# A graph kernel in two layers: window 0 weighed ahead of the weights, and another order for the last two windows of layer 1

## The reference

```python
# layer 0: attention over the edges, 4 heads of 16, with h = relu(layernorm(x))
ZU = einsum('nd,kdr->knr', Z, U)
logits = (ZU[:, src] * ZU[:, dst]).sum(-1) / sqrt(R)
alpha = softmax of logits over the edges of one target
agg = segment_sum(alpha * ZU[:, src], dst)
ssa = einsum('k,knr,kdr->nd', softmax(head_w), agg, U)
...                         # two products with Dmat, relu
x = x + that
# layer 1: h = relu(layernorm(x))
msg = h[src] + relvectors[kind]
red = segment_sum(msg, dst)
x = x + gru_cell(red, h, w_ih, w_hh, b_ih, b_hh)
```

## Time and profile before

| | us |
|---|---|
| median of three runs | 1041.13 |
| the three runs | 1041.29, 1037.07, 1041.13 |
| the profiled execution, its own time | 1040.8 |
| its span | 1038.9 |

### The profile page before, as it was taken

How to read it: one execution, slowest core, us unless ns; L and a number is a source line. 1 busy time by engine, 2 the same in 40 slices (tenths; PEclk the granted TensorE clock), 3 DMA queues, 4 the chain that set the end, 5 groups by cost and what they waited for, 6 DMA issues and landing times.

```text
span 1038.9 us, 14242 instructions
## 1 busy us (share of the span) xinstructions
PE 875.4 (84%) x4828; PEld 686.0 (66%) x4828; DVE 633.3 (61%) x1285; ACT 416.4 (40%) x804; POOL 626.1 (60%) x969
## 2 busy tenths in 40 slices
PE   6833688897888977888888966689999999999996
PEld 5732676776777755777777754466666776777774
DVE  5341577799977777877777744443233433388853
ACT  5423216565655545555565543322211111124441
POOL 4698888888888888888888888881010010000000
PEclk9956557689886777866786887856999999999999
DMA  9361335545655544544454443313344344421111
GB/s 200 70 166 37 77 70 132 130 118 143 158 150 123 118 119 116 139 118 118 120 137 121 118 101 90 92 43 83 105 137 127 122 120 136 125 84 50 51 51 37
DMA packets 54646, 112.99 MB, mean 109 GB/s; under 512 B 15435, under 2 KB 32968, under 8 KB 51443
## 3 DMA queue, kind: packets, MB, share of 16 engines
q1 hardware_dynamic: 34632, 81.38, 24.2%
q0 software_dynamic: 18880, 30.57, 17.8%
q10 hardware_dynamic: 1056, 0.07, 0.1%
HBM read 80.99 MB, written 30.86 MB: 108 GB/s over the span
## 4 chain that ended last, share of the span: by engine, by line
POOL 54%; PE 34%; issue 7%; DVE 1%; SPq 1%; DMA 1%; ACT 1%; ACTq 0%; POOLq 0%; DVEq 0%
POOL shared L725 27%; POOL zs_third L725 13%; POOL cnt_rows L730 13%; PE bank L1957 13%; PE bank L1956 6%; PE bank L1983 5%; PE bank L1984 2%; PE bank L1833 1%; PE bank L1883 1%; PE bank L1934 1%; PE bank L1808 1%; PE bank L1711 1%; PE bank L1980 1%; PE bank L1975 1%; DMA xs<-in_x 1%
## 5 line engine op out<-in xcount | busy, mean ns | idle before, releaser
L725 POOL DMA_INDIRECT shared<-zu_table,src_col x306 | 301.2, 984 | 52.0 <-issue 48.8
L1808 PEld LDWEIGHTS bank<-zus,shared 125*128 125x128 f32 x900 | 148.1, 260 | 15.9 <-issue 14.4
L1808 PE MATMUL bank<-zus,shared 125*128 125x64 f32 x900 | 148.8, 345 | 8.8 <-ACT shared L1519 5.9
L725 POOL DMA_INDIRECT zs_third<-zu_table,src_col x144 | 141.0, 979 | 23.0 <-issue 23.0
L1000 DVE TENSOR_TENSOR setup<-iota_b,bank 128x500 bf16<-128x500 bf16 (+1 forms) x252 | 139.9, 607 | 8.1 <-PE bank L1920 7.9
L1833 PE MATMUL bank<-layer,oh 128*125 128x84 f32 x900 | 144.2, 338 | 0.0
L730 POOL MEMSET cnt_rows<- 54x240 f32 x450 | 142.6, 317 | 0.3
L1833 PEld LDWEIGHTS bank<-layer,oh 128*125 128x125 f32 x900 | 141.6, 254 | 0.3 <-issue 0.3
L1920 PE MATMUL bank<-setup 128*125 128x125 bf16 x450 | 52.2, 253 | 39.7 <-DVE setup L1000 38.8
L1574 ACT ACTIVATE setup<-bank 125x500 bf16<-125x500 f32 (+1 forms) x126 | 77.5, 678 | 12.2 <-PE bank L1920 11.5
L1920 PEld LDWEIGHTS bank<-setup 128*125 128x125 bf16 x450 | 45.9, 164 | 53.4 <-DVE setup L1000 47.0
(11 more groups left out here) (235 smaller groups left out, 1692.2 us busy)
## 6 DMA issues: line engine op xcount, KB each, us to landing
shared<-in_edges SPq DMA_DIRECT2D x25, 1125.0 KB
counts_table<-setup SPq DMA_DIRECT2D x18, 683.6 KB
own_table<-own_out SPq DMA_DIRECT2D x25, 375.0 KB
shared<-own_table SPq DMA_DIRECT2D x25, 375.0 KB
zus<-counts_table POOLq DMA_DIRECT2D x9, 683.6 KB, 5.3
shared<-counts_table POOLq DMA_DIRECT2D x9, 683.6 KB, 5.0
shared<-zu_table,src_col POOLq DMA_INDIRECT x306, 3.9
h_table<-h2s SPq DMA_DIRECT2D x25, 125.0 KB
```

The source lines that it names most:

```text
L725: nc.gpsimd.indirect_dma_start(out=zs[t % 3][:, j * KR:(j + 1) * KR], out_offset=None, in_=zu_table, in_offset=bass.IndirectOffsetOnAxis(a ...
L1808: last = mm(ps(c, 128, (j - a) * KR, (j - a + 1) * KR), ohT[:, j * 128:(j + 1) * 128], zus[:, t, :], start=True, stop=True)
```

## The change

- **The start.** `attend_first` takes the place of `attend(0)`. It weighs window 0 and adds its means before the GRU weights are turned; weights, relation products and biases stand behind. SyncE loads the rows of group 1 (windows 5 to 11) right behind window 0, then windows 1 and 2, then the weights. The edge rows of groups 2 and 3 are loaded in halves in windows 2 to 5 and turned behind `attend(4)` and `attend(6)`. The keys are turned in banks 5, 6 and 7, where they were turned in 0, 1 and 2.
- **The end.** `attend_next_to_last(23)` and `attend_last(24)` have orders of their own on PE, DVE and ACT. VectorE finishes window 23 (its sums divided, its means, the new x, the shift) ahead of chunks 1 and 2 of the logits of window 24. TensorE puts blocks 0 to 17 of the sums of window 0 of layer 2 into window 23, and the others into window 24.
- **For that,** the counts of window 0 have a buffer of their own, `first_many`, loaded by SyncE behind the prefetch for window 24. The sums of windows 0 and 1 go to banks 0 and 1, and the third gate of window 22 goes to the half of bank 6 that is free. GpSimd waits for the last gathers of window 24 before it loads the counts of window 1.

```diff
+        first_many = narrow(part(W, SPAN, SPAN))
...
+            def load_first_counts():
+                sp.wait_ge(oht_made, NW - 1)
+                sp.wait_ge(st_counts, 32 * AHEAD)
+                for lo, hi in SIXTEENTHS:
+                    sp.dma_start(first_many[lo:hi, :], counts_table[lo:hi, :]).then_inc(l_first, 16)
...
                 load_window(0, 0)
+                load_rows(sp, 1, early_rows, GROUPS[1][1])
                 load_window(1, 1)
+                load_window_behind(0, 0)
                 load_gru()
-                load_rows(sp, 1, early_rows, GROUPS[1][1])
-                load_rows(sp, 2, *GROUPS[2])
-                load_rows(sp, 3, *GROUPS[3])
...
-                load_counts(0)
+                pool.wait_ge(g_zs[(NW - 1) % 3][2], 16 * (CHUNKS[2][1] - CHUNKS[2][0]) * ((NW - 1) // 3 + 1))
                 load_counts(1)
...
+            def attend_next_to_last(t, h):          # VectorE
+                differ(t)
+                weigh_rows(t, h)
+                find_cuts(t // 2 + h, 1 - h)
+                one_hots(t + 1, 1 - h)
+                logits(t + 1, t // 2 + h, 1 - h, 0)
+                shift(t - 1)
+                dve.wait_ge(agg_made, t + 1)
+                weigh(t, ps(5, W, 0, SUMS))
+                remainder(t - 1, 1 - h)
+                keep_means(t)
+                relation_one_hots(t + 1)
+                rest_of_rows(t - 1)
+                renew(t)
+                shift(t)
+                logits(t + 1, t // 2 + h, 1 - h, 1)
+                remainder(t, h)
+                logits(t + 1, t // 2 + h, 1 - h, 2)
+                scan(t + 1, 1 - h)
+                find_most(t + 1)
+                rest_of_rows(t)
...
+            def attend_next_to_last(t):             # TensorE
+                pe.wait_ge(x1_made, 2 * t - 1)
+                dense_part(t)
+                target_rows(t + 1)
+                sum_rows(t, t % 2)
+                turn_own(t - 1)
+                sum_blocks(0, 0, 2)
+                turn_means(t)
+                sum_blocks(0, 2, 3)
+                add_means(t)
+                turn_row(t + 1)
+                sum_blocks(0, 3, 4)
+                pe.wait_ge(x1_made, 2 * t + 1)
+                all_own_products(t - 1)
+                sum_blocks(0, 4, 9)
+                turn_logits(t + 1)
+                sum_blocks(0, 9, 13)
+                turn_most(t + 1)
+                sum_blocks(0, 13, 18)
+
+            def attend_last(t):
+                pe.wait_ge(hTw_kept, t + 1)
+                sum_rows(t, t % 2)
+                pe.wait_ge(own_kept, 2 * t - 2)
+                dense_part(t)
+                turn_own(t - 1)
+                turn_means(t)
+                sum_blocks(0, 18, 19)
+                add_means(t)
+                all_own_products(t - 1)
+                sum_blocks(0, 19, NW)
+                pe.wait_ge(own_kept, 2 * t)
+                turn_own(t)
+                sum_blocks(1, 0, 5)
+                all_own_products(t)
```

More of the change, by code:

```diff
@@ L485, in fives_of, with sum_bank, own_third @@
             return i * NW // 5, (i + 1) * NW // 5
-        def overlapped(step):
-            for t in range(NW):
-                step(t, t // 2, t % 2, t == 0, t == NW - 1)
+        def sum_bank(t):
+            return (5, 7)[t % 2] if t >= 2 else t
+        def own_third(t):
+            return ps(6, W, D, 2 * D) if t == NW - 3 else ps(2, W, 0, D)
         def way(eng, windowed, by_blocks):
@@ L1090, in first_logits, with columns_as_numbers @@
             def first_logits():
-                for c in range(3):
-                    logits(0, 0, 0, c)
+                logits(0, 0, 0, 0)
+                columns_as_numbers(1)
+                logits(0, 0, 0, 1)
+                logits(0, 0, 0, 2)
                 scan(0, 0)
                 find_most(0)
-            def attend(t, i, h, first, last):
+            def columns_as_numbers(g):
+                a, b = GROUPS[g]
+                dve.wait_ge(l_rows[g], 16 * (b - a))
+                block = late_rows[:, (a - FIRST) * 128:(b - FIRST) * 128]
+                nc.vector.tensor_copy(block, block.bitcast(int32)).then_inc(v_rowf, 1)
@@ new lines, in attend_first @@
+            def attend_first():
+                differ(0)
+                weigh_rows(0, 0)
+                find_cuts(0, 1)
+                one_hots(1, 1)
+                logits(1, 0, 1, 0)
+                dve.wait_ge(agg_made, 1)
+                weigh(0, ps(5, W, 0, SUMS))
+                keep_means(0)
+                relation_one_hots(1)
+                renew(0)
+                biases()
+                dve.wait_ge(v_bias, 3)
+                three_parts(bfull[:, :], bias3, 0)
+                logits(1, 0, 1, 1)
+                logits(1, 0, 1, 2)
+                scan(1, 1)
+                find_most(1)
+                dve.wait_ge(a_relw, 3)
+                three_parts(relw_low[:, :], low3, 5)
@@ L1111, in attend @@
                     pairs_of(t - 1, 1)
-                if not last:
-                    logits(t + 1, i + h, 1 - h, 2)
+                logits(t + 1, i + h, 1 - h, 2)
                 dve.wait_ge(agg_made, t + 1)
                 weigh(t, ps(5, W, 0, SUMS))
-                if not first:
-                    remainder(t - 1, 1 - h)
-                if not last:
-                    scan(t + 1, 1 - h)
+                remainder(t - 1, 1 - h)
+                scan(t + 1, 1 - h)
                 if pairs:
@@ L1462, in cuts, with exponentials @@
                 nc.scalar.activation(cutf[:, h, 1:HALO], cut[:, h, 1:HALO], ACT.Copy, scale=-BIG).then_inc(cut_made, 1)
-            def attend(t, i, h, first, last):
+            def exponentials(t):
                 act.wait_ge(dif_made, t + 1)
@@ L1493, in attend @@
                     keep_staged(t - 1, 2)
-                if not last:
-                    keep_turned(t + 1)
+                keep_turned(t + 1)
                 if counts:
@@ L1828, in attend, with all_own_products, sum_rows @@
+            def all_own_products(t):
+                relation_products_of_own(t)
+                for c in range(CH):
+                    own_products(t, c)
+            def sum_rows(t, h):
                 pe.wait_ge(oh_made, t + 1)
@@ L1967, in gru @@
                 more = t + 1 < NW
-                sum_blocks(t, LEAD if t else NW - 1, NW)
-                if more:
+                if t:
+                    sum_blocks(t, LEAD, NW)
+                if t and more:
                     sum_blocks(t + 1, 0, 5)
```

311 lines of the change are left out of this document (181 added, 130 removed).

## The result

The changed kernel takes 1030.29 us, median of seven runs (1027.24 to 1050.65); the kernel before took 1041.01, median of seven in the same comparison (1037.07 to 1041.29). The ratio is 0.9898, with a 95% interval of 0.986 to 0.9936: 1.0% faster, where I had forecast 0.25% and put 1038.5 us. The range, 1026.5 to 1043, holds the time, but only by the part of it that rival A had been given: the forecast's own range, 1036.5 to 1042, does not.

What follows compares the result with a forecast made beforehand. GpSimd's gathers bound layer 1, TensorE layer 2. Start 0; end steps -1.1 us (741.4 against 742.53), a load +0.5, an earlier clock -1.5: -2.1 from 1040.8, about 1038.5 us, range 1026.5 to 1043.

Steps and rivals of the forecast that it cites:

- rival A: End of layer 1: clock full from about 690, first GRU begins at 729.3, 13.2 us sooner, 1027.6 us; chance 0.22.
- What bounds the kernel: Layer 1 runs as long as GpSimd needs for 450 gathers; TensorE bounds layer 2, going block to block without a gap.
- the start: Window 0 brought forward, weights, biases and edge rows behind it: gains nothing while GpSimd sets the pace, 0 us (-1 to +1).
- within 1 us of 703: Sign for the start: GpSimd's last gather still ends there; if sooner, the reading of the start is wrong.
- The steps at half clock up to the first turning: Steps 1 to 6 at the end of layer 1: first GRU begins at 741.4 against 742.53, -1.1 us.
- The two transfers: Count loads near the last gathers: GpSimd's moved away, 1.4 us sooner but worth nothing at half clock; SyncE's added, +0.5 us.
- a clock that rises sooner: End of layer 1: full clock 3 us before the guess in the logits' turning is worth -3 us; taken as -1.5.
- the end of the account: The comparison stopped at the first GRU, begun at 742.53 before; work behind it was taken as the same in both kernels.
- if layer 2 loses its dense row of blocks to late loads: Sign that the forecast is wrong, at the start of layer 2; no size given.
- the likeliest case: The forecast itself, with half clock at the end of layer 1: 1037 to 1041.5 us, chance 0.5.
- B: Clock comes back at about 709, amid the logits' turning; GRU begins at 737.9, -4.6 us, 1036 us; chance 0.15.
- C: VectorE's order is the bound, clock half until about 728; GRU begins at 746 to 747, +4, 1045 us; chance 0.1.

Runs made afterwards that it cites:

- paced pair: Kernel before and changed kernel, each with a second clearing of the idle rows behind each of 450 gathers: 1196.14 us and 1186.49 us.
- paced_start: The changed start with the order of before at the end, plus a second clearing of idle rows behind each gather: 1195.57 us, six runs.
- paced_after: The whole changed kernel plus a second clearing of idle rows behind each gather: 1186.49 us, six runs.
- paced_before: The kernel before plus a second clearing of idle rows behind each gather: 1196.14 us, six runs.
- again: The changed kernel rerun with no edit, for another profile: 1205.3 us against 1199.17 of the kernel before on chip 2, ratio 1.0196.

## Why the prediction came out as it did

**What bounds the kernel, and the start: right.** GpSimd waited for no window, and the start is worth 0.6 us in the paced pair, within the scatter. The last gather ended 1.1 us sooner (1.4 in paced_start), which by my own sign ("within 1 us of 703") would speak against this reading. It doesn't: the gathers were shorter one by one (439.8 us in sum for 442.2), and GpSimd had no wait before that could have gone away.

**The steps at half clock up to the first turning: right to about 1 us each.** The profile after is such a run. Counted from the division of window 23: last logits after 8.3 us (720.41; forecast 9.4), their turning after 12.3 (12.7), from there to the division of window 24 8.7 (8.8), to the first turning 12.8 (13.6). Together -2.4 us against before; the forecast had -1.1.

**The two transfers: wrong sign or nothing.** Counts loaded beside the last gathers cost nothing: in the paced pair the last chunk is taken 2.54 us after the last gather with them (859.06 to 861.60) and 2.53 without (857.59 to 860.12). SyncE's load of the first counts did not delay window 23 either: in the profile after it goes out at 677.86 only, and VectorE takes window 23's last chunk at 678.30. For that chunk VectorE waited 0.25 us in the profile after, where 1.30 before, and 0.93 in paced_after, where 2.08 in paced_before. My +0.5 for it was nothing. The -1.5 for a clock that rises sooner was nothing either: it rose 10.4 us after the division of window 23 (712.08 to 722.5), just as guessed (706.3 to 716.7).

**What failed first: the end of the account.** I compared the moment of the first GRU turning and called everything behind it the same in both kernels. It isn't: T1 to T2 is 14.2 to 14.7 us instead of 11.4 in every profile with the new end and the old loads. I named it ("if layer 2 loses its dense row of blocks to late loads") and did not price it, though the trace of before had what it takes: the last h2 store is issued at 730.87, its landing lets the loads out at 736.53, and VectorE comes to them at 747.27. With it, and with the T2 to T3 and the tail of those profiles, half clock is a loss of 3.7 us from D22 on, not the gain of 1.1; about 2 us of loss without the tail, which is not the order's.

**What failed second: the likeliest case.** I took the half clock of the one profile as the usual state at the end and gave rival A 0.22. Rival A named the mechanism that carries the gain, window 23 summed and divided while the last gathers land, and its size: T1 13.2 us sooner; the paced pair shows 13.4 (895.69 to 882.30). Less 3.0 for the late loads (T1 to T3: 25.7, 22.7) and 1.6 in the tail, that is the 8.8 us between the two spans (1192.1, 1183.3). A's 1027.6 us lies among the four shorter times, but that it fits so well is luck: A left the late loads out as well, and with their 3.0 us it gives 1030.6. Its condition, too, I had put too narrowly as "the clock is full from about 690": in the paced pair the old kernel has its clock at half until 868.2, behind 14 us in which its order leaves TensorE idle, and the new one has it back at 857.5, so a part of the gain comes through the clock. How large that part is was not separated. Rivals B and C did not come out as cases of their own. The profiled run is 6.0 us late at D22 and loses 3.7 from there.

**The clock.** I had weighed the rule of the Trainium skill that sustained activity releases the throttled clock (TensorE: Matmul & The Clock Gate, The HAM clock gate). The profile after speaks against it again, more strongly: TensorE is busy for 97 to 100% of each 20 us from 620 to 720 and stays at 0.50. The paced kernel before, on the other hand, returns to full at 868.2, 6 us after work came back at 862.3.

**What stays open.** Why three of the seven times of the change are above 1040; the one of them that was profiled has half clock from 603.1 to 722.5. Of the changed end alone, one profile has a stretch of 105.8 us (794.3 to 900.1) and the other none over 71.7; of the changed start alone, neither profile has one over 47.8. No run here turned it on or off. Open too is that the four shorter times are 10.7 to 13.8 us below the kernel before, and the paced pair shows 9.7: none of the four was profiled.

## What to carry to other kernels

Where one engine sets the pace by feeding others, ask of the last item what the others could finish while they wait for it, and put that ahead of the wait in each queue; it pays by what they would otherwise idle, and in the paced pair the clock was full again sooner as well. Price the change to the end of the first stage behind it: a stage that begins sooner needs its loads sooner, and a load that is issued behind a store's landing does not move by itself. And test such a change under the pace that it was meant for; where another engine is the bound, the same code showed nothing.

## What the runs showed of the hardware

- In one condition (chips 2 and 10 on record, though the last four runs on chip 2 don't show it) TensorE got its matmuls out only one to three at a time, 0.72 or 1.43 us apart, with "issue" as the reason, while GpSimd issued a gather each 1.43 us. The kernel before takes 1195 to 1199 us there instead of 1040. In "again" such idle time of TensorE (over 0.15 us at a time) comes to 92.6 us in 71 places while the gathers run. In the 18 stretches of over 3 us in which GpSimd waits for a window (140.3 us in all) it has one such place of 3.1 us, and behind the last gather none; in the first comparison's two profiles there is none at all. So the stalls go with the gathers, and with something that the other condition lacks. What that is was not tried.
- A second clearing of 54x240 elements behind the first costs GpSimd 0.31 us and a few hundredths between (0.66 for the pair), not another issue gap: 156 us for 450.
- A store to memory and the load that waits for its landing: issued 7.1 us apart in the profile after, and the h2 rows come 8.6 us after their load was issued (748.82 to 757.46 in its chain). It is 6.8 to 7.2 us in all seven profiles with the new end and the old loads, and 5.7 in all four with the old end. There the store of the own gates goes out 1.4 us ahead of it, not 0.3; whether that is the reason was not tried.
